# Placing batch 0's expert rows in two float32r passes instead of one fp32 product

## The reference, cut to what matters

```python
x = x + tanh(g_xattn[0]) * mamba(ctx_1024, layernorm(x), ...)
x = x + tanh(g_ffn[0])   * moe(layernorm(x), ...)        # the expert stage
x = x + tanh(g_xattn[1]) * cross_attention(layernorm(x), ctx_1024, ...)
x = x + tanh(g_ffn[1])   * bitlinear_ffn(layernorm(x), ...)
```

```python
xin = zeros((E, CAP + 1, Hd)).at[eid, slot].set(x[tok]);  inp = xin[:, :CAP]
h   = silu(einsum('ech,ehi->eci', inp, wg)) * einsum('ech,ehi->eci', inp, wu)
out = einsum('eci,eih->ech', h, wd)
g   = out_pad[eid, slot] * (w * valid)[:, None]
y   = zeros((T, Hd)).at[tok].add(g)
```

## Time and profile before

| what | value |
|---|---|
| median of 3 runs | 617.84 us (613.68, 617.84, 635.01) |
| profiled execution, first to last instruction | 612.1 us (no other time of it is given) |
| PE busy | 495.7 us, 81% |
| DVE busy | 478.0 us, 78% |
| ACT busy | 349.4 us, 57% |
| expert stage, first gate product to last placing | 213.6 to 302.8 us |
| mean granted TensorE clock | 0.918 of full |

### The profile page before, as it was taken

The page is one execution under the profiler, slowest core; times in us unless marked ns, Lnnn a source line. Parts: engine busy times, 40 slices in busy tenths (PEclk is TensorE's granted clock), DMA queues, the critical chain, the costliest instruction groups (busy, mean ns, idle before and its releaser), DMA issues.

```text
span 612.1 us, 10074 instructions
## 1 busy us (share of the span) xinstructions
PE 495.7 (81%) x3003; PEld 367.9 (60%) x3003; DVE 478.0 (78%) x1298; ACT 349.4 (57%) x785; POOL 280.9 (46%) x264
## 2 busy tenths in 40 slices
PE   6917777878699389999879999998799988997723
PEld 3302222323288257676679899987689878995602
DVE  4899999999859557987446765895899869756865
ACT  2775554545158132221347666679665996798453
POOL 4129777788010454550048638832776233323211
PEclk9958999979889599999969999999899999999866
DMA  6929100000015399994232103300223000000000
GB/s 165 224 69 376 24 1 0 1 34 1 9 35 176 88 269 299 287 291 140 77 138 70 36 2 70 62 9 2 36 51 70 1 2 1 19 1 1 2 17 17
DMA packets 43816, 48.60 MB, mean 79 GB/s; under 512 B 5644, under 2 KB 40054, under 8 KB 43510
## 3 DMA queue, kind: packets, MB, share of 16 engines
q1 hardware_dynamic: 39926, 36.46, 20.7%
q0 software_dynamic: 3840, 11.54, 8.0%
HBM read 41.43 MB, written 6.56 MB: 78 GB/s over the span
## 4 chain that ended last, share of the span: by engine, by line
PE 33%; DVE 24%; issue 21%; ACT 11%; POOL 8%; DMA 3%; DVEq 1%; SPq 0%; POOLq 0%; ACTq 0%
DVE hst L1670 7%; PE ps L1426 5%; PE ps L1369 4%; PE ps L1370 4%; PE ps L1371 4%; PE ps L1415 3%; DVE hc L1679 2%; DMA G<-token_rows,idx_x 2%; POOL dbu L501 2%; PE ps L1289 2%; ACT pr L860 2%; PE ps L1326 2%; POOL G L580 1%; POOL G L558 1%; DVE ebuf L1806 1%
## 5 line engine op out<-in xcount | busy, mean ns | idle before, releaser
L596 POOL TENSOR_TENSOR pn<-pr,pinv 128x512 f32<-128x512 f32 x64 | 67.6, 1058 | 92.8 <-DVE pinv L2029 92.2
L501 POOL TENSOR_TENSOR dbu<-du,brow 128x512 f32<-128x512 f32 x64 | 81.4, 1282 | 42.0 <-DVE du L1663 23.2
L1122 PE MATMUL ps<-hc,ident 128*128 128x512 f32 x128 | 76.6, 690 | 27.6 <-DVE hc L1679 26.0
L1670 DVE TENSOR_TENSOR_SCAN hst<-ps,dbu 128x512 f32<-128x512 f32 x64 | 77.5, 1211 | 0.2 <-POOL dbu L501 0.2
L722 ACT ACTIVATE ps<-dtv,amat 128x510 f32<-128x510 f32 x64 | 44.1, 690 | 49.2 <-DVE hst L1670 48.3
L860 ACT ACTIVATE pr<-ebuf,smin 128x256 f32<-128x256 f32 x128 | 63.7, 502 | 12.1 <-DVE smin L2020 6.2
L1426 PE MATMUL ps<-pT,cS 128*128 128x256 f32 x256 | 67.4, 386 | 0.0
L558 POOL DMA_INDIRECT G<-token_rows,idx_x x32 | 39.9, 1246 | 57.7 <-DVE wkv L1815 28.5
L1122 PEld LDWEIGHTS ps<-hc,ident 128*128 128x128 f32 x128 | 21.9, 206 | 67.1 <-DVE hc L1679 63.2
L580 POOL DMA_INDIRECT G<-expert_out,idx_g x48 | 51.7, 1078 | 11.6 <-issue 10.2
L1369 PE MATMUL ps<-xnT,mqk 128*128 128x256 f32 x128 | 47.8, 374 | 6.9 <-DVE qT L1995 4.1
(11 more groups left out here) (346 smaller groups left out, 1374.9 us busy)
## 6 DMA issues: line engine op xcount, KB each, us to landing
wdn<-in_L_ffn_wd SPq DMA_DIRECT2D x15, 384.0 KB, 10.3
wgu<-in_L_ffn_wg SPq DMA_DIRECT2D x14, 384.0 KB, 6.3
wgu<-in_L_ffn_wu SPq DMA_DIRECT2D x14, 384.0 KB, 8.5
expert_out<-xn SPq DMA_DIRECT2D x16, 256.0 KB, 4.5
wq<-in_L_xattn_Wq SPq DMA_DIRECT2D x1, 2048.0 KB, 9.3
wo<-in_L_xattn_Wo SPq DMA_DIRECT2D x1, 2048.0 KB, 15.1
wo<-in_L_ffn_w SPq DMA_DIRECT2D x2, 1024.0 KB, 7.4
x<-in_x SPq DMA_DIRECT2D x1, 1024.0 KB, 6.7
```

What stands on the lines that cost most here:

```text
L501: nc.gpsimd.tensor_tensor(dbu[:, j, :], du[:, j % 2, 512 * hb:512 * hb + 512], brow[:, j // 2, :], ALU.mult).then_inc(pool_dbu, 1)
L596: nc.gpsimd.tensor_tensor(pn[:, h % 2], pr[:, h % 2], pinv[:, h % 2, :].unsqueeze(2).to_broadcast([P, 2, L]), ALU.mult)\
L1122: pe.matmul(bank(2 + j % 2), ident[:], hc[:, j % 2, :], start=(isinstance(m, int) and m + k == 0), stop=(isinstance(m, int) and m + k == N ...
L1670: V.tensor_tensor_scan(hst[:, j, :], bank(j % 2), dbu[:, j, :], 0.0, ALU.mult, ALU.add)\
```

## The change

`place` becomes float32r (it holds only zeros and ones, so nothing is lost). ACT rounds each group's `eo` to float32r (`eo_hi`, `rounded_out`), DVE subtracts to get the exact rest (`eo_lo`, `low_out`), and PE places both parts: eight float32r matmuls a group instead of four fp32 ones. `eo_hi` lies over `w1T` and `eo_lo` over `w2T`, so ACT's ternary copies now wait for the last placings and go in the order 0, 2, 1, 3. Two semaphores are saved at the start of the program by sharing counts (`wink_ready`, `in_done`); the instructions there stay as they were.

```diff
+        with ExitStack() as place_scope:
+            place = sb("place", [P, 2, 2, L], F32R, place_scope)
         xn = sb("xn", [P, NT, H])
...
+            def rounded_out(g):
+                act.wait_ge(eo_ready, g + 1)
+                A(eo_hi[:, g % 2], eo[:, g % 2], ACT.Copy).then_inc(eo_hi_ready, 1)
+
             turn(0)
             turn(1)
             gate(0)
             for g in range(NG):
+                if g > 1:
+                    rounded_out(g - 2)
                 if g + 2 < NG:
                     turn(g + 2)
                 if g + 1 < NG:
                     gate(g + 1)
                 turned_rows(g)
-
-            for k in range(4):
+            rounded_out(NG - 2)
+            rounded_out(NG - 1)
+
+            for k in (0, 2, 1, 3):
+                act.wait_ge(summed, NG + k % 2)
                 act.wait_ge(wternT_in_psum, k + 1)
...
-                pe.wait_ge(eo_ready, g + 1)
+                pe.wait_ge(eo_lo_ready, g + 1)
                 for q in range(2):
                     for tt in range(2):
-                        last = pe.matmul(ps[:, 7, H * tt:H * tt + H], place[:, g % 2, q, P * tt:P * tt + P],
-                                         eo[:, g % 2, q, :], start=(g + q + tt == 0),
-                                         stop=(g == NG - 1 and q + tt == 2))
+                        for n in range(2):
+                            last = pe.matmul(ps[:, 7, H * tt:H * tt + H], place[:, g % 2, q, P * tt:P * tt + P],
+                                             (eo_hi, eo_lo)[n][:, g % 2, q, :], start=(g + q + tt + n == 0),
+                                             stop=(g == NG - 1 and q + tt + n == 3))
...
+            def low_out(g):
+                dve.wait_ge(eo_hi_ready, g + 1)
+                V.tensor_tensor(eo_lo[:, g % 2], eo[:, g % 2], eo_hi[:, g % 2].bitcast(F32), ALU.subtract)\
+                    .then_inc(eo_lo_ready, 1)
+
...
                 if g + 2 < NG:
                     slot_shares(g + 2)
+                if g > 0:
+                    low_out(g - 1)
+                if g + 2 < NG:
                     gated(g + 2)
...
                 placed(g)
                 take_out(g)
+            low_out(NG - 1)
```

More of the change, by code:

```diff
@@ L161, in build_program @@
         mqk = [m[:].rearrange("p n (a b) -> p n a b", a=2) for m in mqk]
+        with ExitStack() as high_scope:
+            eo_hi = sb("eo_hi", [P, 2, 2, H], F32R, high_scope)
         w1T = sb("w1T", [P, 2, FI], BF16)
+        with ExitStack() as low_scope:
+            eo_lo = sb("eo_lo", [P, 2, 2, H], F32R, low_scope)
         w2T = sb("w2T", [P, FT, H], BF16)
@@ L229, in build_program @@
         wgu_more = G[:].rearrange("p a k h -> p (a k h)")[:, RING * 2 * ROW:].rearrange("p (a e i) -> p a e i", a=2, e=GROUP)
-        place = xn[:, 0:4, :].rearrange("p (a q) t -> p a q t", a=2)
         spare = sb("spare", [P, 2])
@@ L284, in build_program @@
         consts_ready, zeros_ready = sem("consts_ready"), sem("zeros_ready")
-        wink_ready = sem("wink_ready")
         ctxT_in_psum, winT_in_psum, smallT_in_psum = sem("ctxT_in_psum"), sem("winT_in_psum"), sem("smallT_in_psum")
@@ L288, in build_program @@
         conv_done, u_ready = sem("conv_done"), sem("u_ready")
-        in_done, taps_done = sem("in_done"), sem("taps_done")
+        taps_done = sem("taps_done")
         xdbl_done, split_high = sem("xdbl_done"), sem("split_high")
@@ L318, in build_program @@
         hT_ready, down_done, eo_ready = sem("hT_ready"), sem("down_done"), sem("eo_ready")
+        eo_hi_ready, eo_lo_ready = sem("eo_hi_ready"), sem("eo_lo_ready")
         d_gath = [[sem(f"d_gath{cc}{half}") for half in range(2)] for cc in range(2)]
@@ L689, in _ @@
                   bias=convb[:, 1:2]).then_inc(u_ready, 1)
-                act.wait_ge(conv_done, hb + 1)
+                act.wait_ge(conv_done, 2 + hb + 1)
                 A(u[:, 0, 512 * hb:512 * hb + 512], bank(hb), ACT.Silu, bias=convb[:, 0:1]).then_inc(u_ready, 1)
@@ L1052, in _ @@
             pe.transpose(ps[:, 4, 0:P], win[:, 1, :], ident[:]).then_inc(winT_in_psum, 1)
-            pe.wait_ge(wink_ready, 1)
+            pe.wait_ge(zeros_ready, 3)
             for k in range(NCONV):
@@ L1061, in _ @@
                 pe.matmul(bank(2 + hb), winT[:, 1, 0, :], ctxT[:, 2 * hb:2 * hb + 2, PAD:], start=True, stop=True)\
-                    .then_inc(in_done, 1)
+                    .then_inc(conv_done, 1)
             def conv(hb):
@@ L1581, in _ @@
                 last = V.tensor_scalar(wink[:, 0, k, :], win[:, 0, :], convw[:, 0, k:k + 1], None, ALU.mult)
-            last.then_inc(wink_ready, 1)
+            last.then_inc(zeros_ready, 1)
             def taps(hb, between):
-                dve.wait_ge(in_done, hb + 1)
+                dve.wait_ge(conv_done, hb + 1)
                 found = bank(2 + hb).rearrange("p (b l) -> p b l", b=2)
```

## The result

The changed kernel takes **620.67 us** (median of 7 runs, 619.27 to 621.49). The kernel before, 7 runs beside it, takes 614.62 (613.68 to 635.01). The ratio is 1.0088, 95% interval [1.0059, 1.0117]: slower by about 0.9%, inside the 2%. The forecast of 622.0 is as close as it is by luck: two errors cancel. Its working gave +4.3 us, and the profiled executions differ by 618.2 - 612.1 = +6.1, 1.8 more; but it stood on a median of three runs (617.84) that seven runs put 3.2 lower. What has to be explained is 6.1 against 4.3.

What follows compares the result with a forecast made beforehand. PE bounds the kernel now (5.21 us a group), DVE after the change (5.33). Stage terms +3.8 and +0.4 with a shorter ending put the last placing 3.5 us later; tail +0.8: 617.8 + 4.3 = 622 us, range 614 to 628.

Steps and rivals of the forecast that it cites:

- PE's part: Placing in the expert stage: eight float32r matmuls take 1.12 us a group instead of 1.92, making PE's group 4.41 us.
- DVE's part: Expert stage: ACT's rounding and DVE's subtraction make one DVE-bound group grow by 1.0 us, to 5.33 us with choice slots.
- The take-out of group 2: Early expert stage: added work falls into DVE's waits, so this take-out at 234.9 us is unmoved.
- The sum to group 12: Ten groups from group 2's take-out: +10 x 1.0 us, less 6.2 us of vanishing DVE waits, net +3.8 us.
- The last three groups: Groups 13 to 15: +3.7 us of added DVE work, less 3.3 us of earlier idling for PE, +0.4 us.
- The tail: Behind the last placing: three ternary copies on ACT instead of two delay the copy that starts attention by about +0.8 us.
- The end: Attention to kernel end: attention runs on PE and starts with the turned rows, so the +4.3 us shift reaches the end.
- The first rival: Expert stage: PE stays the bound and gains, limited to 4.0 us by the writes, 614 us; chance 12 in 100.
- the last but one rival: Expert stage: PE's idling lowers the granted clock for two to three groups, +9 us, 631 us; chance 3 in 100.
- one of the prediction's signs of being wrong: Expert stage: the forecast counts as wrong if the granted clock drops inside the stage.
- `placed`: DVE's comparison: float32r output costs 0; the rival that it loses its fast mode, +3.2 us, 625 to 626, 10 in 100.
- The last rival: Placing: two passes no faster than fp32, PE's group 7.1 us, 30 us more, 648 us; chance 2 in 100.

Runs made afterwards that it cites:

- experiment 2: Changed kernel with the added rounding, subtraction and waits kept, but the placing plain fp32 again on unsplit rows: 619.5 us, ratio 1.0101 to the kernel before.
- experiment 1: Changed kernel without ScalarE rounding and DVE subtraction; both float32r placing passes read rows rounded by the take-out: 609.59 us, ratio 0.9937 to the kernel before.
- experiment 5: Changed kernel with ACT rounding straight from PSUM, not waiting for DVE, whose take-out waits for ACT: 615.35 us, ratio 1.0013 to the kernel before.
- experiment 6: Changed kernel with ACT's table load and context copies moved ahead of the four ternary copies: 619.74 us, ratio 1.007 to the kernel before.
- the fastest kernel: Changed kernel, ACT rounding from PSUM and taking out full rows, table load ahead of ternary copies, three row buffers: 608.67 us, ratio 0.9878 to the kernel before.
- experiment 7: Changed kernel, ACT rounding from PSUM and taking out full rows: 613.66 us; with experiment 6's reordering (the tail) 612.16; plus a third row buffer 608.67.

## Why the prediction was right, and where it was off

The mechanism forecast is the one measured: DVE, not PE, sets the group, with ACT's rounding in its chain. The sizes, in the order of the working:

- **PE's part** held: 1.05 us a group against 1.12, since the first matmul behind fp32 work follows by 0.22 to 0.23 us, not by the 0.31 of the earlier trace rows.
- **DVE's part** held nearly to the number: the rounding takes 0.63 us (0.62 taken), the subtraction starts at +1.57 (+1.55), the gated product at +2.27 (+2.25), a group takes 5.33 us. On the rounding's price, 0.63 us lies between the 0.62 taken and the 0.64 that the prediction worked out from the Trainium skill, VectorE: DVE Perf Modes, section on the TRN2 errata. Beside the copy of the same shape from PSUM in the same stretch (0.629 against 0.578 us on average) the SBUF source costs 0.05 us more, nearer the 0.04 estimated from the cycle counts in that section of the Trainium skill than my 0.02. That the cause is DVE's queue with ACT's rounding in its chain is shown from three sides: experiment 2 (the time stays without faster matmuls), 1 (PE's 4.45 us come out when the feeding is gone) and 5 (the period falls by the 0.4 us of the wait).
- **The take-out of group 2, "as unmoved", failed**: it starts at 235.69 us instead of 234.92, +0.77. Ahead of it PE waited for gathered rows that were asked for at the same time (222.6 us) and landed at 230.02 instead of 229.26. The scatter of single executions is as large: in experiments 2 and 6, where DVE and ACT have the change's instructions in the change's order up to there, this take-out starts at 234.76 and 236.08. So the 0.77 can't be put down to the change.
- **The sum to group 12**, +3.8, measured +4.3: 10.3 us added instead of 10.0, and 6.0 of waits gone instead of 6.2. With the first 0.77 the take-out of group 12 is 5.05 us late (295.15 against 290.10).
- **The last three groups**, +0.4: measured +0.47 (304.20 - 295.15 = 9.05 against 298.68 - 290.10 = 8.58). From the last take-out to the end of the placing it is 3.38 us, as forecast (2.26 + 1.12); but before it was 302.62 - 298.68 = 3.94 and not 4.1. The working set a start against the end of a record there (302.8), so 0.7 us shorter became 0.56.
- **The tail**, +0.8: measured 5.65 - 4.96 = 0.69, and experiment 6 gives 0.7 back. The ternary copies and the table load on ACT are what the copy waits for. The working left out PE's clock: at the transposes it was 0.50, which alone would have made the copy 0.45 us late.
- **The end.** 5.65 us at the copy of `xnT`, and 6.1 at the end of the span. Attention gives 0.3 back: the copies of its first heads into `oT`, at 324.70 and 327.42 us before and 330.05 and 332.77 now, are 5.35 late. The rest lies in the kernel's last product, for which the granted clock was 1.00 before and 0.56 now, 0.76 us:

```profile
607.88 1.03 PE L1521 MATMUL ps<-w2T,wdn 128*128 128x256 bf16 x8 [0.35 <-ACT wdn L955]
```

```profile
613.24 1.79 PE L1536 MATMUL ps<-w2T,wdn 128*128 128x256 bf16 x8 [0.35 <-ACT wdn L969]
```

  It takes 1.03 us in experiment 2 as well and 1.87 in the fastest kernel, so this 0.76 is not a cost of the two passes. Together 0.77 + 0.5 + 0.07 + 0.14 - 0.11 - 0.3 + 0.76 = 1.8, the difference between 6.1 and 4.3; about 1.5 of it are the late gather and the last product.
- **The first rival** was bounded wrongly. "Its best price is limited", 4.0 us, since the writes "land at about 280 us whatever PE does". The quick execution of experiment 1 ended its placing 8.6 us earlier, with a single wait of 1.7 us for a write, in spite of full DMA engines (share 1.06 from 240 to 270 us). The flaw: full engines until 280 us bound the sum of the traffic, not when one write lands; in that stretch it landed in 3.7 us in experiment 1, and a third buffer lets it be late. The point at which this rival was to be decided, the take-out of group 4, went against it: 250.77 us, where 248.9 was its sign and 250 the forecast. Had DVE had room, the range's lower end of 614 would have been too high, as 609 and 608.67 show.
- **The clock** did what the last but one rival says, in small. The working had set against it that every idle stretch stays near 1 us; the longest was 3.0, ahead of the placing at 245.54, and behind it the granted clock is 0.50, the level of 1.2 GHz, for 3.4 us. In experiment 2 a wait of 1.8 us ahead of the same placing was followed by 3.2 us at 0.51. So one of the prediction's signs of being wrong came, a drop inside the stage. It cost nothing there: DVE was busy for 3.33 of the 3.4 us, and this group took 7.55 us from take-out to take-out, the one before it, with the same work on DVE, 7.53. The window:

```profile
246.20:249.60 3.40, 3.40 (x21) 2.65 (x21) 3.33 (x4) 0.00 (x0) 2.67 (x2) 0.50 1.05 312
```

- **`placed`** kept its speed: 0.60 us for two with the float32r output, 0.61 before.
- **Two slips** in the working moved no term of the sum. The last rival says eight matmuls at 0.24 us; that is 1.92, what the fp32 placing takes already, and its 7.1 us a group and 648 us belong to eight at 0.48. And the clock before was not 1.00 throughout the stage: the earlier trace rows give 0.97 from 214 to 240 us.

## What to carry to other kernels

Before making the busiest engine faster, count what the second one has left in a group without waits (here 4.33 of 5.21 us) and what the feeding of the new form puts there, in work and in waits on a third engine; a saving of 0.8 us a group was lost to 1.0 us of that. A conversion that hangs between two engines is better read from the common source by both (0.4 us a group here), and the work it adds belongs on the engine with room: ACT had it. When that is done, look again at the buffers: with two, DVE waited only 3.3 us in ten groups at 5.2 us a group, and when PE's period of 4.45 came in reach a third was worth about 3.5 us (612.16 to 608.67).

## What the runs showed of the hardware that was not expected

- ACT and DVE each took scaled rows out of PSUM as float32r or fp32 at nearly the same price, 128x256 in 472 to 479 ns on ACT (kernels of experiments 5 and 7) and in 479 on DVE, so moving the take-out costs ACT no more than it frees on DVE.
- A transfer's time to land is no constant of its size. From 240 to 290 us the same 256 KB write took, in the median, 6.1 us in the kernel before, 5.0 in the change, 3.7 in experiment 1, 9.5 in the kernel of experiment 7 with two buffers and the tail, and 8.6 with three, `xn`'s two. The DMA issues of that stretch in the kernel with two buffers and the tail, then in experiment 1 (count, KB each, median us to landing):

```profile
expert_out<-xn SPq DMA_DIRECT2D x9, 256.0 KB, 9.5
```

```profile
expert_out<-eo SPq DMA_DIRECT2D x11, 256.0 KB, 3.7
```

What made them 9.5 us was not settled.

- The granted clock differs between executions at the same place, and single traces differ by it: the last product of the kernel took 1.03 us at 1.00 (before, experiment 2) and 1.79 at 0.56 (the change), and the transposes ahead of attention 0.66 or 1.11.
